# Two attention layers of a megakernel: the row-maxima pass of batch 1 interleaved with the value pass of batch 0, and one load per local head instead of three

## The reference

```python
# layer 0: sliding window of 64, keys of the chunk before and of the own chunk
scores = einsum('bhnid,bhnjd->bhnij', qc, kc) / sqrt(16)
mask = band & (kv_global >= 0)          # j >= i, j <= i + 64
out = softmax(where(mask, scores, min)) @ vc
# layer 1: one key/value head shared by 16 query heads, strictly causal
scores = einsum('bhtd,bsd->bhts', q, k) / sqrt(16)
out = softmax(where(pos_k < pos_q, scores, -1e30)) @ v     # row 0 gives zeros
```

## Time and profile before

| What | Value |
|---|---|
| Median of 3 runs | 715.74 us (710.91 to 716.55) |
| The profiled execution itself | 715.33 us |
| Its span in the profile | 713.5 us, 11274 instructions |
| Mean granted TensorE clock | 0.955 of full |
| PE busy / PEld busy | 633.7 us (89%) / 545.0 us (76%) |
| DVE / ACT / POOL busy | 389.9 (55%) / 294.0 (41%) / 144.3 us (20%) |
| DMA | 48.92 MB, mean 69 GB/s |

### The profile page before, as it was taken

The page is one execution under the profiler, slowest core; times in us unless marked ns, Lnnn a source line. Parts: engine busy times, 40 slices in busy tenths (PEclk is TensorE's granted clock), DMA queues, the critical chain, the costliest instruction groups (busy, mean ns, idle before and its releaser), DMA issues.

```text
span 713.5 us, 11274 instructions
## 1 busy us (share of the span) xinstructions
PE 633.7 (89%) x3990; PEld 545.0 (76%) x3990; DVE 389.9 (55%) x730; ACT 294.0 (41%) x435; POOL 144.3 (20%) x142
## 2 busy tenths in 40 slices
PE   4989788859899999999999696779987799999995
PEld 3878677757788888888888575667667688888884
DVE  6378144676745544544457779952337633334455
ACT  4466255323443333343331743435660534433331
POOL 5411024403522222222220000001123032222220
PEclk9999799978999999999999999978999699999999
DMA  8444366310011111111100030412221001111101
GB/s 319 112 164 177 93 165 174 98 45 0 24 44 45 53 56 44 44 44 44 44 22 1 4 118 18 136 51 64 76 91 45 0 23 45 44 45 44 44 22 59
DMA packets 27199, 48.92 MB, mean 69 GB/s; under 512 B 4672, under 2 KB 9184, under 8 KB 27168
## 3 DMA queue, kind: packets, MB, share of 16 engines
q1 hardware_dynamic: 26848, 48.38, 22.1%
q10 hardware_dynamic: 320, 0.13, 0.1%
HBM read 36.57 MB, written 11.93 MB: 68 GB/s over the span
## 4 chain that ended last, share of the span: by engine, by line
PE 71%; DVE 12%; ACT 4%; SPq 4%; DMA 4%; issue 3%; POOL 1%; DVEq 0%; ACTq 0%
PE PS L492 33%; PE PS L831 15%; PE PS L700 3%; PE PS L723 3%; PE PS L736 3%; DVE nmx L1299 3%; PE PS L636 2%; DMA qk_slot<-k_scr 2%; PE PS L553 1%; SPq L318 1%; DVE stats L1207 1%; PE PS L789 1%; PE PS L702 1%; DVE xn L1369 1%; DVE x L1373 1%
## 5 line engine op out<-in xcount | busy, mean ns | idle before, releaser
L492 PE MATMUL PS<-h_hi,wqkv_hi 128*128 128x512 f32 x352 | 122.3, 407 | 4.0 <-POOL wqkv_hi L456 2.1
L1080 ACT ACTIVATE qk_hi<-xn 128x512 fp32r<-128x512 f32 x82 | 51.8, 632 | 178.0 <-DVE xn L1481 138.8
L492 PE MATMUL PS<-h_hi,wqkv_lo 128*128 128x512 f32 x336 | 113.7, 396 | 0.0
L1478 DVE TENSOR_TENSOR pr<-pr,PS 128x512 f32<-128x512 f32 x60 | 41.3, 688 | 86.8 <-PE PS L492 86.8
L492 PEld LDWEIGHTS PS<-h_hi,wqkv_hi 128*128 128x128 f32 x352 | 68.6, 195 | 19.4 <-POOL wqkv_hi L456 2.3
L1483 DVE TENSOR_TENSOR qk_lo<-xn,qk_hi 128x512 fp32r<-128x512 f32 x74 | 51.2, 692 | 52.7 <-ACT qk_hi L1080 52.7
L492 PE MATMUL PS<-h_lo,wqkv_hi 128*128 128x512 f32 x184 | 74.7, 406 | 0.0
L492 PEld LDWEIGHTS PS<-h_hi,wqkv_lo 128*128 128x128 f32 x336 | 63.5, 189 | 13.5 <-issue 0.3
L1076 ACT ACTIVATE pr<-PS 128x512 f32<-128x512 f32 x82 | 48.8, 596 | 43.0 <-PE PS L492 42.8
L831 PE MATMUL PS<-wqkv_hi,qk_hi 128*128 128x256 f32 x336 | 62.1, 284 | 3.3 <-POOL qk_lo L462 1.7
L456 POOL TENSOR_TENSOR wqkv_hi<-fw_raw,wqkv_hi 128x768 fp32r<-128x768 f32 x21 | 40.9, 1948 | 113.3 <-ACT wqkv_hi L1069 113.3
(11 more groups left out here) (209 smaller groups left out, 1346.3 us busy)
## 6 DMA issues: line engine op xcount, KB each, us to landing
fw_raw<-in_ffn SPq DMA_DIRECT2D x41, 384.0 KB, 3.0
qk_slot<-q_scr SPq DMA_DIRECT2D x64, 132.0 KB
q_scr<-qk_hi SPq DMA_DIRECT2D x16, 256.0 KB
q_scr<-qk_lo SPq DMA_DIRECT2D x16, 256.0 KB
qk_slot<-k_scr SPq DMA_DIRECT2D x64, 64.0 KB
wmod<-in_wmod SPq DMA_DIRECT2D x1, 1536.0 KB, 13.4
x<-in_x SPq DMA_DIRECT2D x2, 512.0 KB, 4.2
wmod<-in_wmod SPq DMA_DIRECT2D x1, 1024.0 KB, 9.5
```

Source lines behind the costliest of these rows:

```text
L492: ins = nc.tensor.matmul(dst, left(a, c), right(b, c), start=n == 0, stop=n == total - 1)
L1080: nc.scalar.activation(hidR[b][0], hid[b], ACT.Copy).then_inc(f["hi"], 1)
L1478: tt(hid[b] if half is None else gu[b], gact[b], PS[:, 5, :], ALU.mult).then_inc(f["gu"], 1)
```

## The change

Three things change, in both layers.

1. The last 8 units of the maxima pass (units 24 to 31; `LEAD` = 8 units of batch 1 stay in the pass) move into the value pass: before `keys_major(u)` for u < 8, PE runs `scores` of unit 24 + u. These "alone" units use one set of banks only (banks 0 and 1 in layer 0, 0 to 2 in layer 1), `keys_major` takes the others: two sets in layer 0 (banks 2 to 5), a single set (banks 3 to 5) for units 0 to 7 in layer 1. ACT and DVE interleave alike: ACT masks units 28 to 31 after exponentials 0 to 3; DVE takes a unit's maxima before its share of `outputs`. `max_rows(1)` and what follows it come after `keys_major(8)`. In layer 0 `shifts_rest0` and `gates(0)` now stand before the value pass, behind 24 units of scores.
2. SP stores batch 0 and its maxima first and starts to load at once; the stores of batch 1 follow between loads, after units 3, 5, 7, 9 (layer 0, four 256 KB stores each) and 3, 6 (layer 1; after unit 6 also the keys and the loads of `k1` for batch 1).
3. In layer 0 queries and keys of a unit lie side by side in one DRAM array `qk0_scr[unit][row][query or key][512]`, with the keys stored twice and the ones stored once; one DMA of 264 KB per unit takes the place of three (132 KB and twice 64 KB). POOL's four fills with ones go.

```diff
+MAX_BANK = [[4, 0], [6, 6]]
+LEAD = 8
+STORES = [[3, 5, 7, 9], [3, 6]]
...
+        qk0_scr = nc.dram_tensor("qk0_scr", [UNITS, ROWSM, 2, S], F32, kind="Internal").ap()
...
+        def key_bank(l, u):
+            if l == 0:
+                return 2 + 2 * (u % 2)
+            return 3 if u < LEAD else 3 * (u % 2)
...
+            def store_rows0(b, i):
+                m = ORDER0[b][i]
+                u = b * H + 8 * (m % 2)
+                for part, done in ((0, qhi), (1, qlo)):
+                    sp.wait_ge(done, 4 * b + i + 1)
+                    src = qkR[part][:, m, :].bitcast(F32)
+                    for row in ((2 * part, 2 * part + 1), (part, part + 2))[m // 2]:
+                        sp.dma_start(qk0_scr[u:u + 8, row * DH:(row + 1) * DH, m // 2, :], src)\
+                            .then_inc(scr0_written[m], 16)
...
             def load_keys_major(l, u):
                 s = u % SLOTS
                 if u >= SLOTS:
                     sp.wait_ge(at[l]["st"], u - 3)
-                sp.dma_start(qk[s][0:ROWSM, 0:S].bitcast(F32), q_scr[l][u, :, :]).then_inc(at[l][f"qk{s}"], 16)
+                both = qk[s][0:ROWSM, :].bitcast(F32).rearrange("p (a c) -> p a c", c=S + WIN)
                 if l == 0:
-                    rows = k0_scr[u, :, :, :].rearrange("r d t -> (r d) t")
-                    for half in range(2):
-                        sp.dma_start(qk[s][half * ROWS // 2:(half + 1) * ROWS // 2, S + WIN:].bitcast(F32), rows)\
-                            .then_inc(at[l][f"qk{s}"], 16)
+                    sp.dma_start(both[:, :, 0:S], qk0_scr[u, :, :, :]).then_inc(at[l][f"qk{s}"], 16)
+                else:
+                    sp.dma_start(both[:, 0, 0:S], q1_scr[u, :, :]).then_inc(at[l][f"qk{s}"], 16)
             def load_attention(l):
+                store_maxima(sp, l, 0)
+                for u in range(UNITS):
+                    if u % H == 0:
+                        sp.wait_ge(at[l][f"mw{u // H}"], 16 * 2)
+                    if l == 0 and u % H == 0:
+                        for m in range(4):
+                            sp.wait_ge(scr0_written[m], 16 * 4 * (u // H + 1))
+                        sp.wait_ge(ones_written, 16)
+                    load_keys_major(l, u)
+                    if l == 0 and u in STORES[0]:
+                        store_rows0(1, STORES[0].index(u))
+                    if l and u in STORES[1]:
+                        store_queries1(1, STORES[1].index(u))
+                    if l and u == STORES[1][-1]:
+                        store_keys1(1)
...
             def scores(l, g, s, b):
+                alone = isinstance(u, int) and u >= H + LEAD
...
-                        bank, col = 2 * (s % 2) + t // 2, (t % 2) * KEYS0
+                        bank, col = (0 if alone else 2 * (s % 2)) + t // 2, (t % 2) * KEYS0
                         if t % 2 == 0:
-                            ge(a["mxd"], 2 * (u - 2) + t // 2 + 1)
+                            ge(a["mxd"], 2 * (u - 1 if alone else u - 2) + t // 2 + 1)
...
+                    if alone:
+                        pe.wait_ge(a["mxd"], 3 * (u - 1) + bank + 1)
...
             def keys_major(l, u):
-                if u >= 2:
-                    pe.wait_ge(a["p"], u - 1)
+                if u:
+                    ge(a["p"], u - 1 if first != key_bank(l, u - 1) else u)
+                if u == 0:
+                    pe.wait_ge(a["mxd"], (2, 3)[l] * (H + LEAD))
...
             def values_pass(l):
-                for s in range(2):
-                    keys_major(l, s)
                 if l == 0:
                     shifts_rest0()
                     gates(0)
-                pe.wait_ge(at[l]["mlo"], B)
-                if l == 0:
+                    pe.wait_ge(modT_taken, 2)
                     pe.wait_ge(gate_taken, 2)
...
+                for u in range(UNITS):
+                    if u < LEAD:
+                        scores(l, BQ + (LEAD + u) // SLOTS, u % SLOTS, 1)
+                    if l and u % H == 0:
+                        pe.wait_ge(k1_loaded, 16 * 2 * (u // H + 1))
+                    keys_major(l, u)
+                    if u == LEAD:
+                        pe.wait_ge(at[l]["oe"], 1)
+                        max_rows(l, 1)
+                    if u >= SLOTS and u % SLOTS == 1:
+                        values(l, u // SLOTS - 1)
                 values(l, QUADS - 1)
...
             def attention(l):
                 if l == 0:
+                    gates(0)
                     act.wait_ge(split, 3)
+                act.wait_ge(qlo, (4 * B, 4 * B + 3 * B)[l])
                 for u in range(UNITS):
                     exponentials(l, u)
-                    if l == 0 and u == 1:
-                        gates(0)
+                    if u < SLOTS:
+                        mask_q(l, 1, BQ + BQ - 1, u)
+                    if u == LEAD:
+                        max_high(l, 1)
...
             def outputs_pass(l):
-                for g in range(QUADS):
-                    outputs(l, g)
+                for u in range(UNITS):
+                    if u < LEAD:
+                        maxima(l, BQ + (LEAD + u) // SLOTS, u % SLOTS)
+                    if u == LEAD:
+                        max_low(l, 1)
+                    if u >= SLOTS and u % SLOTS == 1:
+                        outputs(l, u // SLOTS - 1)
+                outputs(l, QUADS - 1)
```

More of the change, by code:

```diff
@@ L630, in scores @@
                     return
[L631 removed]
+                if not alone:
+                    ge(a["mxd"], 3 * (u - 1))
                 for qt in range(NT):
                     bank, col = BANK1[qt]
[L634 removed]
+                    if alone:
+                        pe.wait_ge(a["mxd"], 3 * (u - 1) + bank + 1)
+                    else:
+                        bank += 3 * (s % 2)
                     diagonal = WIDTH1[qt] - qt * P
```

189 lines of the change are left out of this document (89 added, 100 removed).

## The result

| | Median, us | Runs | Ratio to before, 95% interval |
|---|---|---|---|
| Before, on the same chip | 713.41 | 4 (710.91 to 716.55) | |
| After | 728.49 | 4 (727.01 to 734.88) | 1.027 (1.020 to 1.034) |

The change made the kernel slower, by 2.7% in the ratio and by 2.1% in the medians. The forecast was 705.8 us, with 698 to 714 as its range; the time is 14.5 us above the range's upper end. The profiled execution took 727.01 us (span 725.2, mean granted clock 0.937 in place of 0.955, 51.28 MB by DMA in place of 48.92).

A forecast was written before the change was run, and what follows sets the result against it. Layer 0 was taken as bound by DVE, then SP's issue plus load landing; layer 1 by DVE, then PE, with slow-clock stretches. 715.33 - 4.8 (layer 0) - 6.2 (layer 1) + 1.5 (clock) = 705.8 us; range 698 to 714.

The forecast's parts named there:

- The batch 0 stores ... I price them at 0; ... 0 to 2 us: Layer 0, SP's queue: 16 stores and the ones end near 52 us, cost 0, or 0 to 2 if batch 1's keys wait.
- each group of four batch 1 stores holds SP for 5.0 us ... 5.6 us of new waits: Layer 0's loop: batch 1's stores between loads delay units 8 and 10, adding 5.6 us of waits.
- in layer 0 the waits for loads 8 and 10 absorb it: Clock term, layer 0: low clock after new idle times adds nothing beyond the load waits already counted.
- loads start at 65 to 67: Layer 0: batch 1's maxima issue at 61 us and land after 3.4 to 5.70, so loads start at 65 to 67.
- the modulation ... I take 6.0: Layer 0 before the value pass: modulation matmuls take 6.0 us, nearer full clock (4.7) than half (9.4).
- rival D: Layer 0's gates stay at half clock, 9.4 us instead of 6.0: 709.2 us; chance 0.20 together with A.
- 22 units at 1.40: Layer 0 from unit 10 on: 22 units at 1.40 us each, paced by 264 KB loads at 192 GB/s.
- rival A: Layer 0: the 66-row load is no faster than three loads, 1.62 us a unit: 710.6 us; chance 0.20 together with D.
- -6.2 us: Layer 1: interleaving scores with keys ends the last `values` at 531.1 us against 537.3, a gain of 6.2.
- +1.5: Layer 1: one short stretch of low clock costs 1.5 us; range of this term 0 to 6.
- C: Both interleaved loops run at half clock through short waits, 35.3 us more: 739.6 us; chance 0.10.
- B: New waits halve as stores pass SP in half the time, pace 1.27, no low clock: 696.6 us; chance 0.17.

The follow-up runs named there:

- e1: The changed kernel with the transfer of the ones moved from ahead of batch 0's 16 stores to behind them; 718.8 us, ratio 1.012.
- e9: The changed kernel with the same ones, still ahead of batch 0's stores, read from 32 partitions in place of two; 720.4 us, ratio 1.017.
- e2: The changed kernel with the old scratch, 12 stores a batch and three loads a unit, batch 1's stores still between loads; 712.5 us, ratio 1.006.
- e5: e2 with batch 1's layer 0 stores ahead of the first load, leaving the interleaving in both layers; 706.3 us, ratio 0.997.
- e6: The kernel before with the interleaving in layer 1 alone, layer 0 as before; 708.7 us, ratio 0.997.
- e10: The kernel before plus the two-partition transfer of ones ahead of batch 0's 12 stores, into a scratch nothing reads; 714.0 us, ratio 1.011.
- e3: The kernel before with the joint layout, its 16 stores a batch, ones and one load a unit, without interleaving; 728.7 us, ratio 1.026.
- e4: The changed kernel with batch 1's 16 layer 0 stores ahead of the first load; 725.1 us, ratio 1.021.
- e11: Repeat of e5 with more rounds: the kernel before with the interleaving in both layers; 706.7 us, ratio 0.998.
- e12: Repeat of e6 with more rounds: the kernel before with the interleaving in layer 1 alone; 707.7 us, ratio 0.997.
- e7: The changed kernel with the joint load cut to 64 rows, a second load for two rows of maxima, no ones stored; 718.5 us, ratio 1.012.
- e8: e7 with batch 1's 16 layer 0 stores ahead of the first load; 714.9 us, ratio 1.007.

## Why the prediction was wrong

Against the forecast's own times layer 0 ran late as follows: the first pair of scores and keys began at 77.76 in place of 72.5 (5.3 us), unit 8 at 104.73 in place of 92.9 (11.8), unit 10 at 111.93 in place of 98.7 (13.2), and the last `values` ended at 148.5 in place of 130.9 (17.6). So 5.3 us were lost ahead of the loop, 7.9 in it up to unit 10, and 4.4 in the 22 units behind.

**Step "The batch 0 stores ... I price them at 0; ... 0 to 2 us".** This failed first. The bound was set by how long SP needs for 16 issues at 1.24 us. The transfer of the ones was named and got no price. Its shape held the stores behind it at 58 to 105 GB/s. Measured: the first scores of batch 1 5.3 us late (57.56 to 52.27, e1), the end of layer 0 6.8 us late, 9.7 us by the medians, and the same start regained by a change of shape alone (e9, 8.1 us by the medians).

**Step "each group of four batch 1 stores holds SP for 5.0 us ... 5.6 us of new waits".** The place was right, the mechanism only in part. SP did hold the loads: 6, 8 and 10 left about 1.9, 4.1 and 1.6 us after their slots were free (from 74.34 four stores took 3.77 us of SP, and not 5.0, since the first two took 1.23 together). But the larger part is the landing, taken as 3.5 us. The four groups, 4 MB in all, were in flight with 264 KB loads (219 GB/s from 92.5 to 113.0), and from their issue to PE's use loads 6, 8 and 10 took 8.4, 9.7 and 10.9 us. The three waits named above sum to 7.46 us, against 5.6. What was missing is the clock: 0.71 over that stretch, in which PE did 106 matmuls in 20.5 us. The step "in layer 0 the waits for loads 8 and 10 absorb it", which priced the clock at nothing in layer 0, failed: PE's matmuls came back from these waits at half clock (0.50 from 97.8 to 108.0 and from 111.9 to 118.2). With the old layout the stores' place was worth 6.2 us (e2 against e5).

**"loads start at 65 to 67".** 69.94, because batch 1's scores began 5 us late. In e1, without that, the first load left at 64.32.

**"the modulation ... I take 6.0".** 1.87 + 3.70 us, with their overlap 5.4: better than forecast, and rival D did not happen. All nine profiles with the interleaved order of layer 0 have this, so the step held. Part of the gain was no gain against the kernel before, though, since two of five profiles with the old order (e6, e10) have the same.

**"22 units at 1.40".** From 123.25 to 142.00 three quads of the changed kernel took 6.25 us each, 1.56 a unit, and over all 22 units the step fell short by 4.4 us. That is rival A's case, that 66 rows in one load move no faster than three loads. Its 1.62 was read from one quad of before; the six from 92.56 to 130.16 take 6.27 in the mean, 1.57 a unit. In the chain a load landed 4.96 to 5.23 us after its issue. From the third to the seventh `values` a quad took 6.06 to 6.59 us in the five profiles with the joint load of 66 rows (after, e1, e3, e4, e9), 5.71 to 6.15 in the seven with three loads (before, e2, e5, e6, e10, e11, e12), 5.60 and 6.10 in the two with 64 rows (e7, e8). So the joint load bought nothing in the loop and may have cost a little. The row of 192 GB/s behind the 1.40 was a burst. By the rule of the Trainium skill (DMA: Bandwidth & Descriptors, section Why a DMA increments its semaphore by 16 and not by 1) 66 rows run on 11 engines and 64 on 16. e7 against e1 agrees in the pace of the loop (5.60 against 6.16 us), though the time of the kernel is the same.

**Layer 1, "-6.2 us", clock "+1.5".** Near in the sum (-3.7 measured against -4.7) and in some parts: in the profile after, layer 1's steady quads took the 7.33 us of before, and the bias wait of 2.2 us came as 2.18. But the sum is near by luck, since the comparison starts from one execution at a clock of 0.55, and e3 and e10, which are without the interleaving, took 124.3 and 124.4 us as well. Against these two the interleaved profiles gained 0.4 us in the mean. Moving the scores saved 1.66 us a unit ahead of the loop and cost 2.69 for a pair in place of 1.26 for keys alone, 1.43 a unit. That leaves 1.8 us for eight units, and the waits at the loop's two ends, 2.18 us at its start, can account for the rest.

**Rivals.** No rival had the time. A's mechanism came true, a pace of the loop no better than before, without its time of 710.6. C named the slow side and the low clock, at 739.6 and with all of both loops at half clock; in layer 0 that came for parts of the loop, 22.3 us of it, behind waits of 2 to 3 us, and in layer 1 it did not, as the pairs ran at 0.82 in the mean. B and D did not happen. That the change's stores and ones, not its order, could be the cost was no rival, though the earlier trace rows showed batch 1's maxima already waiting behind stores.

**The ledger.** From the changed kernel's 728.5: ones out of the way -9.7 (718.8, e1), the rest of the layout, which is the keys stored twice and loaded jointly, -6.3 (712.5, e2), stores ahead of the loads -6.2 (706.3, e5). By the end of layer 0 in the profiles, 148.5, 141.7, 137.5 and 129.8, the three are 6.8, 4.2 and 7.7 us. Each is measured at its place in this order; e4 (-3.4) and e8 (-3.6) show that the stores' place is worth less while the doubled key stores stand ahead of the maxima.

## What to carry to other kernels

Price a small transfer by its shape before its bytes: ahead of other DMAs, one that starts from two partitions held 256 KB stores at a quarter to a half of their rate, and the same bytes from 32 partitions did not. Trading loads for stores (keys stored twice so that one load does) moves cost from a loop, where it was hidden in part, to the queue ahead of the loop's start. And a gain read from a low-clock stretch of one execution should first be looked for in a second execution of the same kernel: both stretches that this forecast meant to save were faster in some executions of kernels in which that code was unchanged (129.2 in place of 135.7 for the end of layer 0 in e6, 124.4 in place of 128.0 for layer 1 in e10).

## What the hardware showed beyond expectation

- Ones from 2 partitions, 128 KB: the stores behind them moved at 105 and 58 GB/s for 6 us, against 203 and 201 behind the same ones from 32 partitions.
- A burst of stores between loads let a 264 KB load land after 10.85 us, at 219 GB/s in sum; once the stores were out, it took 4.96 to 5.23 us.
- One kernel ran the modulation of layer 0 in two executions at different clocks: 3.46 and 6.42 us in e12, 1.86 and 3.70 in e6. Most executions of the kernel before lay between 703.4 and 714.4 us, the faster ones mostly at the higher mean clock (0.962 at 703.4, 0.953 at 714.4).
- The load of 66 rows in one piece landed in 4.67 to 5.42 us (e1), the same one cut to 64 rows and 2 in 3.59 to 4.48 (e7), at 176 and 182 GB/s and DMA shares of 0.61 and 0.75.
